# Head products of 64 columns, and a two-turn exit from PSUM, in a macaron block on one core

## The reference

```
x = x + 0.5 * ffn(layernorm(x));  x = x + attn(layernorm(x));  x = x + 0.5 * ffn(layernorm(x))
ffn(x):  hidden = silu(x @ W1.T) * (x @ W3.T)       # 2048 wide
         out = fwht(hidden) @ W2.T                  # Walsh-Hadamard transform
attn(x): q, k, v = split(rmsnorm(x) @ quant(qkv_w).T)    # 16 heads of 32
  for each chunk of 128 tokens, with a state S per head:
    scores = (q k^T) * mask              # mask: decay below the diagonal
    o      = scale * (scores v + (q * lam_t) S)
    S      = lam_T * S + (k * lam_rev)^T v
  out = rmsnorm(rmsnorm(o)) @ quant(proj_w).T
```

## Time and profile before

| | us |
|---|---|
| median of 3 runs (lowest, highest) | 2385.5 (2384.63, 2386.05) |
| the profiled execution, its own time | 2387.63 |
| its span, first to last instruction | 2385.9 |
| TensorE busy | 2344.0 (98%) |
| VectorE busy | 1199.0 (50%) |
| ScalarE busy | 712.2 (30%) |
| GpSimd busy | 143.6 (6%) |

### The profile page before, as it was taken

One profiled execution on the slowest core, in us unless ns is written; L12 is line 12 of the kernel. 1 busy time (PEld: TensorE's weight loads), 2 busy tenths in 40 slices (PEclk: granted clock), 3 DMA queues, 4 the chain that ended last, 5 costly groups with the idle time before them and its releaser, 6 DMA issues.

```text
span 2385.9 us, 31855 instructions
## 1 busy us (share of the span) xinstructions
PE 2344.0 (98%) x12851; PEld 1121.7 (47%) x12851; DVE 1199.0 (50%) x2145; ACT 712.2 (30%) x1196; POOL 143.6 (6%) x102
## 2 busy tenths in 40 slices
PE   6999999999999999999999999999999999999999
PEld 3444445444444455444544454455445544544444
DVE  6576645554465445545455355534564455444312
ACT  5645333222232332223222332222233213322211
POOL 0090000000000000000000000000000000000000
PEclk9999999999999999999999999999999999999999
DMA  7947531242223322333142133411332223131210
GB/s 198 228 142 190 137 106 45 67 119 54 63 48 113 74 49 62 93 75 85 32 126 60 54 80 81 105 45 36 106 80 69 65 54 98 27 89 29 60 36 18
DMA packets 299460, 196.87 MB, mean 83 GB/s; under 512 B 231601, under 2 KB 256177, under 8 KB 295473
## 3 DMA queue, kind: packets, MB, share of 16 engines
q1 hardware_dynamic: 299024, 194.31, 31.4%
q10 hardware_dynamic: 288, 0.52, 0.1%
HBM read 84.68 MB, written 54.53 MB: 58 GB/s over the span
## 4 chain that ended last, share of the span: by engine, by line
PE 86%; DVE 3%; issue 3%; DMA 2%; POOL 2%; ACT 1%; SPq 1%; DVEq 0%; ACTq 0%; POOLq 0%
PE d_bank L1405 25%; PE l_bank L1385 24%; PE g_bank L1385 24%; PE a_bank L1440 5%; PE a_bank L1423 2%; PE a_bank L1499 2%; PE a_bank L1487 2%; PE a_bank L1451 1%; POOL work L714 1%; PE a_bank L1481 1%; POOL work L713 1%; DVE work L1122 1%; PE a_bank L1465 1%; DMA w1t<-kT 0%; DMA parts_dram<-q_parts 0%
## 5 line engine op out<-in xcount | busy, mean ns | idle before, releaser
L1405 PE MATMUL d_bank<-w2t,work 128*128 128x512 f16 x2940 | 673.7, 380 | 1.5 <-DVE work L1122 1.5
L1102 DVE SCALAR_TENSOR_TENSOR work<-l_bank,l_scale,work 128x512 f32<-128x512 f32 x256 | 191.7, 749 | 574.3 <-PE l_bank L1385 573.9
L1405 PEld LDWEIGHTS d_bank<-w2t,work 128*128 128x128 f16 x2940 | 285.1, 98 | 335.4 <-issue 4.3
L1385 PE MATMUL g_bank<-xt,w1t 128*128 128x512 f16 x1536 | 354.1, 380 | 4.7 <-DMA w1t<-q_parts 1.9
L1385 PE MATMUL l_bank<-xt,w3t 128*128 128x512 f16 x1536 | 352.4, 379 | 1.7 <-DVE work L1102 1.3
L831 ACT ACTIVATE work<-g_bank,g_scale 128x512 f32<-128x512 f32 x256 | 175.4, 685 | 503.5 <-PE g_bank L1385 497.1
L1385 PE MATMUL l_bank<-work,w3t 128*128 128x512 f16 x1344 | 308.4, 379 | 0.2 <-DVE work L1102 0.2
L1385 PE MATMUL g_bank<-work,w1t 128*128 128x512 f16 x1344 | 308.3, 379 | 0.0
L850 ACT CAST work<-work 128x512 f16<-128x512 f32 x232 | 143.3, 618 | 520.7 <-DVE work L1102 519.2
L1385 PEld LDWEIGHTS g_bank<-xt,w1t 128*128 128x128 f16 x1536 | 147.6, 98 | 181.0 <-issue 4.7
L1385 PEld LDWEIGHTS l_bank<-xt,w3t 128*128 128x128 f16 x1536 | 147.6, 98 | 175.7 <-issue 1.8
(11 more groups left out here) (216 smaller groups left out, 1699.6 us busy)
## 6 DMA issues: line engine op xcount, KB each, us to landing
work<-parts_dram SPq DMA_DIRECT2D x192, 128.0 KB, 2.8
x_dram<-work SPq DMA_DIRECT2D x16, 1024.0 KB, 4.6
work<-x_dram SPq DMA_DIRECT2D x11, 1024.0 KB, 7.1
parts_dram<-q_parts SPq DMA_DIRECT2D x32, 256.0 KB, 2.0
parts_dram<-k_parts SPq DMA_DIRECT2D x32, 256.0 KB, 2.2
norm_dram<-cent SPq DMA_DIRECT2D x32, 256.0 KB, 2.0
w2t<-in_L_ffn_W_dram SPq DMA_DIRECT2D x30, 256.0 KB, 3.4
xin<-in_L_attn_x_dram SPq DMA_DIRECT2D x7, 1024.0 KB, 7.6
```

The lines of the kernel that those rows point to most:

```text
L1102: nc.vector.scalar_tensor_tensor(out=hfull, in0=l_bank[:], scalar=l_scale[:, j:j + 1], in1=gate, op0=ALU.mult, op1=ALU.mult).then_inc(hful ...
L1385: ins = nc.tensor.matmul(dst[:], wt[:, wp, k, P * j:P * (j + 1)], src[:, xp, k, :], start=(k == 0 and wp == xp), stop=(k == KT - 1 and wp ...
L1405: ins = nc.tensor.matmul(d_bank[t][:], parts[:, hp, P * t:P * (t + 1)], w2t[:, j, wp, :], start=(j == 0 and hp == wp), stop=(j == HT - 1 a ...
```

## The change

Two things. In a pv step, the high half of the scores of a head now meets both value halves in one product: its moving operand is the head's 32 columns of the high and of the low half (two runs of 32 with a gap), 64 columns in all, and its output goes to two runs of 32 in a PSUM bank. The low half of the scores still meets the high values in a product of 32 columns, which adds to the first run. So each chunk takes 256 columns of the bank in place of 128, as two halves `a`, and the bank holds two chunks.

So the bank is taken and emptied twice for a head group, after chunk 1 and after chunk 3, and each turn takes two instructions: ScalarE scales the first half of both chunks into `x2`, and then VectorE multiplies the second half by the same scale and adds it to `x2`. The waits that named the old turns name the new ones.

```diff
             if step == "pv":
-                return (1, 1) if arg[2] == 0 else None
+                return (1, 2) if arg[2] % 2 == 0 else None
...
             elif step == "pv":
-                USES[step, arg] = USES["pv", arg[:2] + (0,)]
+                USES[step, arg] = USES["pv", arg[:2] + (arg[2] - 1,)]
...   # GpSimd, step q
-                        bank_pv, fill = filled("pv", (b, g - 1, 0))
+                        bank_pv, fill = filled("pv", (b, g - 1, TT - 1))
...   # ScalarE
-                elif step == "pv" and arg[2] == TT - 1:
-                    g = arg[1]
+                elif step == "pv" and arg[2] % 2:
+                    _, g, c = arg
                     b, fill = filled(step, arg)
                     act.wait_ge(a_ready[b], fill)
-                    nc.scalar.activation(x2[:, :, P * g:P * (g + 1)],
-                                         a_bank[b][:].rearrange("p (c e) -> p c e", c=TT), ACT.Copy,
+                    nc.scalar.activation(x2[:, c - 1:c + 1, P * g:P * (g + 1)],
+                                         a_bank[b][:].rearrange("p (c a e) -> p c a e", c=2, a=2)[:, :, 0, :], ACT.Copy,
                                          scale=o_scale[:]).then_inc(a_free[b], 1)
...   # VectorE, step ostat
-                    b, _ = filled("pv", (a, GROUPS - 1, 0))
-                    dve.wait_ge(a_free[b], copied("pv", (a, GROUPS - 1, 0), b) + 1)
+                    b, _ = filled("pv", (a, GROUPS - 1, 2))
+                    dve.wait_ge(a_free[b], copied("pv", (a, GROUPS - 1, 2), b) + 2)
...   # VectorE, new
+                elif step == "pv" and arg[2] % 2:
+                    a, g, c = arg
+                    b, _ = filled(step, arg)
+
+                    dve.wait_ge(a_free[b], copied(step, (a, g, c - 1), b) + 1)
+                    o = x2[:, c - 1:c + 1, P * g:P * (g + 1)]
+                    nc.vector.scalar_tensor_tensor(out=o, in0=a_bank[b][:].rearrange("p (c a e) -> p c a e", c=2, a=2)[:, :, 1, :],
+                                                   scalar=o_scale[:], in1=o, op0=ALU.mult, op1=ALU.add).then_inc(a_free[b], 1)
...   # TensorE, step pv
-                    if c == 0:
+                    if c % 2 == 0:
                         take(step, arg)
+                    halves_o = a_bank[b][:, 2 * P * (c % 2):2 * P * (c % 2 + 1)].rearrange("p (a e) -> p a e", a=2)
...
-                        nc.tensor.matmul(a_bank[b][:, P * c:P * (c + 1)], qdec[:, P * c:P * (c + 1)], state[:, c - 1, :],
-                                         start=False, stop=False, skip_group_check=True)
+                        nc.tensor.matmul(halves_o[:, 0, :], qdec[:, P * c:P * (c + 1)], state[:, c - 1, :],
+                                         start=(c == 2), stop=False, skip_group_check=True)
                     v = values(x2)
                     for h in range(HG):
-                        col = P * c + HD * h
-                        for sp, vp in ((0, 0), (0, 1), (1, 0)):
-                            ins = nc.tensor.matmul(a_bank[b][:, col:col + HD], sc[:, c % 2, sp, h, :],
-                                                   v[:, c, g, vp, HD * h:HD * (h + 1)],
-                                                   start=(c == 0 and h == 0 and sp == vp), stop=True, skip_group_check=True)
-                    if c == TT - 1:
+                        cols = slice(HD * h, HD * (h + 1))
+                        nc.tensor.matmul(halves_o[:, :, cols], sc[:, c % 2, 0, h, :], v[:, c, g, :, cols],
+                                         start=(c == 0 and h == 0), stop=True, skip_group_check=True)
+                        ins = nc.tensor.matmul(halves_o[:, 0, cols], sc[:, c % 2, 1, h, :], v[:, c, g, 0, cols],
+                                               start=False, stop=True, skip_group_check=True)
+                    if c % 2:
                         ins.then_inc(a_ready[b], 1)
```

## The result

The changed kernel takes 2373.38 us in the median (2372.69 to 2375.16, five runs) against 2385.5 before. The two medians are 12.1 us apart, a quotient of 0.9949; the ratio computed over the runs, which isn't the quotient of the two medians, is 0.9944, 95% interval 0.9933 to 0.9955. Forecast were -9.2 us. The sign and the main mechanism came out; the size was a quarter short.

What follows compares the result with a forecast made beforehand. TensorE's dense queue of products, busy 98%, was taken as the bound. Shorter pv steps (-11.3 us) plus bank waits in late groups (+2.1) gave -9.2 us: 2376.3 us from 2385.5, range 2372.7 to 2382.

Steps and rivals of the forecast that it cites:

- The sign: Whole kernel: faster, by 9.2 us; 80% chance of faster by more than the 4.8 us a measurement tells apart.
- main mechanism: TensorE's pv steps: 8 products per step instead of 12, 88 ns less in each of 128 steps, 11.3 us less.
- The bound: From the first attention step on, TensorE's dense queue sets the time; shortening it shortens the run by as much.
- The wide product: In each pv step, a 64-column product takes 28 ns beside 25 for 32 columns: 11.3 us less in all.
- The floor case: Rival, 14%: the 64-column product in pv steps takes 25 ns, like 32 columns: 12.8 us less, 2374.8 us with waits.
- nothing saved: Rival, 8%: the gapped wide product in pv steps works as two, 50 ns: 2386.1 us, no change.
- the slower case: Rival, 9%: writing two runs into PSUM is dearer than the wide product itself: +3 us at 55 ns, up to 2416 us.
- The wait for the bank: At chunk 2, TensorE waits for bank 1 in eight late head groups, 0.26 us each: 2.1 us more.
- The exits: Evictions of 128 x 256 after chunks 1 and 3: 467 ns on ScalarE, 482 ns on VectorE.
- the dear-eviction case: Rival, 10%: evictions cost as much as at 512 columns, late groups wait 0.74 us each, 5.9 in all: 2380.1 us.
- The sum of the terms: Whole kernel: -11.3 us for products plus 2.1 us for waits makes -9.2 us.
- The step that failed: On TensorE's queue: what shortens it shortens the run by as much; fewer products were costed as time, 11.3 us less.

Runs made afterwards that it cites:

- e5: The changed kernel with a head's two halves side by side in PSUM, so the wide product writes 64 adjacent columns: 2374.1 us, ratio to before 0.9945.
- e1: The changed kernel with its wide product split into two products of 32 columns again, both turns out of PSUM kept: 2388.5 us, ratio to before 1.0009.
- p2: The changed kernel with 96 idle products (192 TensorE instructions) added at the very start: 2381.5 us, ratio to before 0.9979.

## Why the prediction was wrong in size

**The bound**: right. TensorE's queue sets the time, and each punctual group gained 4 x 0.0825 = 0.33 us to the end of the run.

**The wide product**: right in kind, a little dear. Forecast 28 + 25 = 53 ns for wide and narrow; measured 28.4 + 26.9 = 55. A step is 82 to 83 ns shorter, not 88: 128 x 0.0825 = 10.6 us for 11.3. The floor case, "nothing saved" and the slower case are out. The latter was the case of the page "PSUM — Partial Sum Buffer" of the Trainium skill; this trace doesn't agree with its sentence for an output of two runs of 32 values, and e5 shows the gap in the output at 0 ns.

**The wait for the bank**: right in place, count and size. 0.13 + 0.10 us in the eight late groups, 1.8 us for 2.1. The exits were priced to 2 ns; the dear-eviction case is out. In three of the late groups TensorE waits for VectorE between chunk 0 and score 2 anyway, and there the first step's gain is lost, 0.25 us.

**The sum of the terms**: -10.6 + 1.8 + 0.25 = -8.5 us. The two traces differ by 12.5 us; without the surplus of the three places that is 7.5, and without the 1.0 us of other single waits that are longer in the changed kernel, 8.5. Forecast for these terms were -9.2.

**The step that failed** is the one that wasn't there: the text said that what shortens TensorE's queue shortens the run "by as much". It costed 512 products and their weight loads as time and not as instructions. They are also 64 KB less of instruction DMA, and the rest of the packets moved. At 623, 669 and 1121 us the kernel before had a packet on top of transfers on whose landing TensorE depends, and the earlier trace rows showed the effect without the cause: single waits of 2.7 and 1.1 us that occur once or twice, in 32 head groups that are all alike. I took such waits as part of the kernel that stays. These places were worth 5.0 us of the 12.5 between the traces (1.7 of them the drop of the clock at 639 us, which e1 did without), and they could have gone the other way: the same change with 192 instructions of another phase (p2) is 7 us slower, -4.4 us in all.

What stays open: why a packet at 623 us delays the other queue by up to 1.9 us where it takes 1.6 itself, which transfers of the first 219 us the phase meets, and what decides whether the clock drops after one of these waits.

## What to carry to other kernels

Price a small product by the distance of starts from rows of neighbouring widths, and an added exit from PSUM by the engine's own slope over columns; both came out to 5% here. Then look for late instances: the wait that a change adds falls only on the groups in which the releasing engine is behind. Where a kernel issues tens of thousands of instructions beside DMAs that are on the path, a change in their number moves the instruction fetches. Here that was worth more than a third of the gain, and with another phase (p2) it took more than half of it away: padded controls (a part of a packet, a whole packet) tell the two apart.

## What the runs showed of the hardware

- Pitch of fp16 products with a 128x128 weight load each: 25 ns at 32 and at 48 columns, 28 at 64, 55 at 128, 216 at 512. Writing two runs of 32 with a gap costs nothing more than 64 adjacent columns (28.4 ns in both, e5). A gap in what is read was in every run of the wide product, so no run isolates it; 28.4 ns is what the line through 128 and 512 columns gives.
- TensorE's instructions come in packets of 16 KB, 256 instructions each, one in 24 us on the mean here (101 in 2386), and transfers that share the time with one land later: the one at 623 us took 1.6 us of one engine, and the q store beside it landed in 9.9 to 10.2 us in place of 8.4 to 8.7.
- After the same wait of 1.8 us TensorE went on at its upper clock level in one execution (granted clock 1.00) and mostly at the lower one in another (0.62), for 12 products of 512 columns: 1.7 us between two runs of like kernels.
